# Two-layer transformer step on one core: modulation's end in item 22, items 29 to 31 reordered, attention transposed sooner, three context projections in the opening

## The reference

```python
# layer 0: 16 heads of 64
attn_in = _adaln(x, cond, ln1_w, ln1_b, g1_w, g1_b, b1_w, b1_b)
x = _attn(attn_in, attn_in, sa_wq, sa_wkv, sa_wo, sa_bo) + x     # with rope on q and k
cross_in = _adaln(x, cond, ln1_w, ln1_b, g1_w, g1_b, b1_w, b1_b)
ctx_n = _ln(context, ca_lnc_w, ca_lnc_b)
x = _attn(cross_in, ctx_n, ca_wq, ca_wkv, ca_wo, ca_bo) + x
ffn_in = _adaln(x, cond, ln2_w, ln2_b, g2_w, g2_b, b2_w, b2_b)
h = jax.nn.gelu(ffn_in @ ff_w1 + ff_b1, approximate=False)
x = h @ ff_w2 + ff_b2 + x
# layer 1: 16 heads of 8
mod = jax.nn.silu(c) @ W_ada + b_ada          # sh_msa, sc_msa, sh_x, sc_x, sh_mlp, sc_mlp
h1 = _modulate(_ln(x), sh_msa, sc_msa)
x = x + (attend(q, k, v of h1 @ W_qkv + b_qkv) @ W_proj + b_proj)
h2 = _modulate(_ln(x), sh_x, sc_x)
ctx = text_embed @ W_ctx + b_ctx
x = x + (attend(h2 @ W_q, ctx @ W_k, ctx @ W_v) @ W_out + b_out)
h3 = _modulate(_ln(x), sh_mlp, sc_mlp)
x = x + (gelu(h3 @ W_fc1 + b_fc1) @ W_fc2 + b_fc2)
```

## Time and profile before

| | us |
|---|---|
| median of three runs (393.54 to 394.5) | 393.87 |
| the profiled execution | 393.85 |
| its span in the profile | 392.1 |
| busy: TensorE | 375.7 (96%) |
| busy: VectorE | 305.3 (78%) |
| busy: ScalarE | 293.4 (75%) |
| busy: GpSimd | 177.5 (45%) |

### The profile page before, as it was taken

How to read it: one execution, slowest core, us unless ns; L and a number is a source line. 1 busy time by engine, 2 the same in 40 slices (tenths; PEclk the granted TensorE clock), 3 DMA queues, 4 the chain that set the end, 5 groups by cost and what they waited for, 6 DMA issues and landing times.

```text
span 392.1 us, 9870 instructions
## 1 busy us (share of the span) xinstructions
PE 375.7 (96%) x3591; PEld 287.5 (73%) x3591; DVE 305.3 (78%) x657; ACT 293.4 (75%) x1022; POOL 177.5 (45%) x156
## 2 busy tenths in 40 slices
PE   7999999999999999999999898999999999999997
PEld 3577777777877777777787577776768778788665
DVE  4779978979888888787898668674758888888751
ACT  2377878878878788777877585789679887987942
POOL 3165547557456665445575224342465650402120
PEclk9999999999999999999999899999999999999999
DMA  7153343223333333332122100000000000000001
GB/s 250 51 181 128 111 131 109 101 83 109 123 120 110 109 110 108 109 114 96 55 82 83 54 30 26 2 2 0 3 2 2 2 3 2 2 2 3 4 0 54
DMA packets 17424, 26.09 MB, mean 67 GB/s; under 512 B 3584, under 2 KB 6272, under 8 KB 17376
## 3 DMA queue, kind: packets, MB, share of 16 engines
q1 hardware_dynamic: 17088, 25.24, 19.0%
q10 hardware_dynamic: 288, 0.22, 0.3%
HBM read 8.67 MB, written 0.52 MB: 23 GB/s over the span
## 4 chain that ended last, share of the span: by engine, by line
PE 71%; DVE 15%; ACT 8%; issue 3%; POOL 2%; DMA 1%; DVEq 0%; POOLq 0%
PE bank L984 57%; PE bank L1065 7%; PE bank L1272 5%; ACT prob L437 3%; DVE nmax L847 2%; ACT raw L523 2%; DVE hT L668 1%; DVE nmax L719 1%; POOL xn L282 1%; DVE st L641 1%; DVE qk L751 1%; PE bank L1311 1%; PE bank L995 1%; DVE xn L656 1%; DVE x L636 1%
## 5 line engine op out<-in xcount | busy, mean ns | idle before, releaser
L301 POOL TENSOR_TENSOR swp<-swp,small 128x512 f32<-128x512 f32 x62 | 78.4, 1279 | 48.1 <-PE bank L984 28.3
L437 ACT ACTIVATE prob<-bank,nmax 128x128 f32<-128x128 f32 x256 | 91.5, 391 | 1.2 <-DVE nmax L719 1.2
L523 ACT ACTIVATE raw<-bank,nmax 128x128 f32<-128x128 f32 x256 | 72.7, 390 | 11.0 <-DVE nmax L847 10.9
L719 DVE TENSOR_REDUCE nmax<-bank 128x4 f32<-128x512 f32 x64 | 41.2, 685 | 29.7 <-PE bank L984 29.7
L437 ACT ACTIVATION_READ_ACCUMULATOR prob<-bank,nmax 128x1 f32 x256 | 59.2, 231 | 0.0
L334 POOL TENSOR_TENSOR prob<-prob,rz 128x512 f32<-128x512 f32 x29 | 30.2, 1041 | 55.1 <-DVE rz L724 55.1
L847 DVE TENSOR_REDUCE nmax<-bank 128x4 f32<-128x512 f32 x64 | 41.2, 684 | 15.4 <-PE bank L984 15.4
L984 PE MATMUL bank<-hT,wqkv 128*128 128x512 f32 x96 | 49.2, 596 | 0.5 <-DVE qk L751 0.5
L443 ACT ACTIVATE probT<-bank 128x512 f32<-128x512 f32 x32 | 19.1, 597 | 35.3 <-PE bank L1065 35.3
L751 DVE TENSOR_TENSOR qk<-bank,small 128x512 f32<-128x512 f32 x64 | 42.8, 670 | 0.9 <-ACT raw L428 0.6
L984 PEld LDWEIGHTS bank<-wqkv,oT 128*128 128x128 f32 x256 | 33.2, 192 | 14.0 <-issue 12.9
(11 more groups left out here) (114 smaller groups left out, 665.9 us busy)
## 6 DMA issues: line engine op xcount, KB each, us to landing
swp<-raw SPq DMA_DIRECT2D x124, 128.0 KB, 2.1
wqkv<-in_wqkv SPq DMA_DIRECT2D x16, 256.0 KB, 2.8
wff<-in_wff SPq DMA_DIRECT2D x4, 256.0 KB, 3.0
x<-in_x SPq DMA_DIRECT2D x2, 256.0 KB, 4.1
wmod<-in_wmod SPq DMA_DIRECT2D x1, 512.0 KB, 6.0
rows<-in_row SPq DMA_DIRECT2D x2, 192.0 KB, 2.4
ctx<-in_ctx SPq DMA_DIRECT2D x1, 384.0 KB, 3.1
ctxT<-in_ctxT SPq DMA_DIRECT2D x1, 384.0 KB, 3.4
```

The source lines that it names most:

```text
L301: nc.gpsimd.tensor_tensor(four(swp[:, m % 2, f, :]), four(swp[:, m % 2, f, :]), sin[f], ALU.mult).then_inc(rope_sin[f], 1)
L437: last = nc.scalar.activation(prob[:, hh, bcols(u)], S[hh][:, bcols(u)], ACT.Exp, bias=nmax[:, s % 2, hh, u:u + 1], accum_out=zsum[:, s % ...
L523: last = nc.scalar.activation(prob1[:, s % 2, hh, bcols(u)], score_bank(s, hh)[:, bcols(u)], ACT.Exp, bias=nmax[:, s % 2, hh, u:u + 1])
L719: nc.vector.tensor_reduce(nmax[:, s % 2, hh, :], four(S[hh][:, :]), AX.X, ALU.max, negate=True).then_inc(rowmax[hh], 1)
```

## The change

- **Modulation**: `modulation_end(1)` moves from item 28 to item 22, where VectorE calls it behind `rope_sum(23)`.
- **Context**: ctx1 of both halves and ck of half 0 are projected in the opening, where two idle matmuls stay of eight. ck of half 1, cv of half 0 and cv of half 1 take items 10, 18 and 26; items 9, 17 and 25 have none. ctxT and the two blocks of wsq that this needs are loaded behind the first half of x, as is now the first block of wmod.
- **Statistics**: of the four bn_stats in items 9, 17 and 25 two move to the next item, ahead of the aggregation.
- **Seam**: `prob_values(28)` and the transposition of item 29 now stand ahead of `down(0, 0, O)`; ScalarE copies item 28's result at the end of item 29; `down` waits for that copy, and the wait for the residual goes to `prob_values(29)`. `rope_sum(31)` moves from item 30 to the end of item 29, and VectorE's copy of transposed probabilities in item 30 between its two row maxima.
- **Attention**: `attention_T` stands ahead of the transpositions in items 11, 19 and 27, and ScalarE's copy of it ahead of the second head's exponentials.

The diff, cut to what is spoken of:

```diff
@@ -164,7 +164,7 @@
             sem(f"ld_{name}") for name in ("small", "tab", "rows", "ctx", "ctxT", "sq", "ff"))
-        ld_mod, ld_swap = pair("ld_mod"), sem("ld_swap")
+        ld_mod, ld_swap, ld_ctxw = pair("ld_mod"), sem("ld_swap"), sem("ld_ctxw")
         ld_wqkv = [sem(f"ld_wqkv{i}") for i in range(2 * RUN)]
@@ -194,10 +194,10 @@
                 ("q", 1), ("k", 1), ("cq", 0), ("cq", 1)]
-        PROJ_BANK = [O, O, O, O, O, O, X, Y, Y, W, S[1], S[1]]
+        PROJ_BANK = [O, W, O, O, O, O, X, Y, Y, W, S[1], S[1]]
         AT = {what: i for i, what in enumerate(PROJ)}
-        PROJ_SLOT = {9: 0, 10: 1, 17: 2, 18: 3, 25: 4, 26: 5}
+        PROJ_SLOT = {10: 3, 18: 4, 26: 5}
@@ -229,10 +229,8 @@
                     load(wqkv[:, s + 3, :], wqkv_in[:, s + 3, :], ld_wqkv[s + 3])
-                elif s == 5:
-                    load(ctxT[:, :, :], ctxT_in.rearrange("d (h t) -> d h t", h=2), ld_ctxT)
-                elif s <= 7:
-                    part = (slice(4 * P, len(SQ) * P), slice(0, 4 * P))[s - 6]
+                elif 5 <= s <= 7:
+                    part = (slice(6 * P, 8 * P), slice(0, 4 * P), slice(4 * P, 5 * P))[s - 5]
                     load(wsq[:, part], wsq_in[:, part], ld_sq)
@@ -243,6 +241,11 @@
             load_x(0)
+            load(wmod[:, 0:2 * P], wmod_in[:, 0:2 * P], ld_mod[0])
+            load(ctxT[:, :, :], ctxT_in.rearrange("d (h t) -> d h t", h=2), ld_ctxT)
+            for name in ("ctx", "ck"):
+                part = slice(SQ[name] * P, (SQ[name] + 1) * P)
+                load(wsq[:, part], wsq_in[:, part], ld_ctxw)
             load(wqkv[:, 0, :], wqkv_in[:, 0, :], ld_wqkv[0])
@@ -484,7 +487,7 @@
             def l0_slot(s):
-                if s >= 2:
+                if s >= 2 and s != 30:
                     evacuate_o(s - 2)
@@ -500,6 +503,8 @@
                     evacuate_v(s + 2)
+                if s == 29:
+                    evacuate_o(28)
                 if s == 28:
@@ -572,14 +577,13 @@
                     scale_shift(3, 1, Y)
+                if s % RUN == 3 and RUN < s:
+                    evacuate_attention(s // RUN - 1)
                 if s < ITEMS and s != 5:
...
             def background1(s):
-                for run in range(3):
-                    if s == RUN * run + 11:
-                        evacuate_attention(run)
                 if s == 3:
@@ -607,10 +611,12 @@
             load(small[:, 0:NFIRST], small_in[:, 0:NFIRST], ld_small)
-            load(wmod[:, 0:2 * P], wmod_in[:, 0:2 * P], ld_mod[0])
             act.wait_ge(ld_small, 16)
             nc.scalar.activation(silu[:, 0, :], condT, ACT.Exp, scale=-1.0).then_inc(exp_c, 1)
+            evacuate_proj("ctx1", 0)
+            evacuate_proj("ctx1", 1)
             scale_shift(0, 0, T[0])
+            evacuate_proj("ck", 0)
             evacuate_v(0)
@@ -636,8 +642,8 @@
-            def ln_stats(k, half):
-                for u in range(HALF):
+            def ln_stats(k, half, first=0, end=HALF):
+                for u in range(first, end):
                     last = nc.vector.bn_stats(st[:, half, u, :], x[:, HALF * half + u, :])
@@ -771,18 +777,22 @@
                 row_max(s, 0)
+                if s == 30:
+                    copy_T0(29)
                 row_max(s, 1)
...
                 middle0(s)
-                if s >= 1:
+                if s >= 1 and s != 30:
                     copy_T0(s - 1)
...
                 normalise(s)
-                if s < 31:
+                if s < 30:
                     rope_sum(s + 1)
+                if s == 22:
+                    modulation_end(1)
                 if s <= 28:
@@ -791,8 +801,10 @@
                 if s in (10, 18):
+                    ln_stats(1, s // RUN - 1, 2, HALF)
                     ln_aggregate(1, s // RUN - 1)
                 if s == 26:
+                    ln_stats(2, 0, 2, HALF)
                     ln_aggregate(2, 0)
@@ -801,7 +813,6 @@
                 if s == 28:
-                    modulation_end(1)
                     scale_shift_last(2, 0, O)
@@ -821,7 +832,7 @@
                     residual(run // 2, run % 2, W, wo_done, RUN * run + RUN)
-                    ln_stats(1 + run // 2, run % 2)
+                    ln_stats(1 + run // 2, run % 2, 0, 2)
                 if s in (10, 11, 18, 19):
@@ -832,6 +843,7 @@
                     ln_aggregate(3, 0)
+                    rope_sum(31)
                 if s == 30:
@@ -1082,7 +1094,7 @@
                     wait_hT(2, 0)
-                if s == 28:
+                if s == 29:
                     pe.wait_ge(x_sum[0], 3)
@@ -1116,8 +1128,10 @@
                 if i == 0:
-                    pe.wait_ge(ld_sq, 32)
+                    pe.wait_ge(ld_ctxw, 32)
                     pe.wait_ge(ld_ctxT, 16)
+                if i == 4:
+                    pe.wait_ge(ld_sq, 48)
                 if what in ("ck", "cv"):
@@ -1188,19 +1202,22 @@
                     fill(s + 2, 2)
-                if s == 29:
-                    background0(s)
                 if s == 31:
...
                     prob_values(s - 1)
+                if s == 29:
+                    prob_values(28)
                 transpose_probs(s, 0)
+                if s == 29:
+                    background0(s)
                 if s == 0:
                     pe.wait_ge(silu_done, 1)
+                    pe.wait_ge(proj_out, 3)
                     modulation(1, O)
-                if 1 <= s < 30:
+                if 1 <= s < 29:
                     prob_values(s - 1)
@@ -1215,7 +1232,7 @@
                 if s >= 2:
-                    pe.wait_ge(o_out, s - 1)
+                    pe.wait_ge(o_out, s if s == 29 else s - 1)
                 if s == 4:
@@ -1351,6 +1368,8 @@
                     project("cq", s // RUN - 1)
+                if s % RUN == 3 and RUN < s:
+                    attention_T(s // RUN - 1)
                 if 1 <= s <= ITEMS:
@@ -1366,8 +1385,6 @@
                         turn_back(2 * run + 1)
-                    if s == e + 11:
-                        attention_T(run)
                 if s == 1:
@@ -1426,8 +1443,11 @@
             modulation(0, Y)
-            keep_warm(8, X)
+            keep_warm(2, X)
+            project("ctx1", 0)
+            project("ctx1", 1)
             transpose_norm(0, 0, [T[0], T[1]])
+            project("ck", 0)
             pe.wait_ge(mod_read, 1)
```

## The result

The changed kernel takes 392.06 us (median of 11 runs, 391.11 to 393.91), the kernel before, beside it, 393.87 (11 runs, 393.54 to 395.94): a ratio of 0.9949, with an interval of 0.9929 to 0.9969. The forecast was 391.4, the range 389.0 to 393.3. The profiled executions have spans of 390.3 us after and 392.1 before, at mean granted clocks of 0.996 and 0.995, and each has one stretch of half clock of some 3.5 us, so they can be held against each other.

What follows compares the result with a forecast made beforehand. TensorE, with 71% of the chain that ends last, was taken as the bound. Terms of -2.6, +0.35, +1.35, -3.55, +0.1, +1.5, +1.3 and -0.9 sum to -2.45: from 393.85 to 391.4 us, range 389.0 to 393.3 (8 in 10).

Steps and rivals of the forecast that it cites:

- Bound: Whole kernel: TensorE carries 71% of the chain; edits count where they remove its matmuls or make or end its stops.
- Projections: Items 9, 17, 25: each loses a context projection of 0.86 us, nothing else being late there; -2.6 us in all.
- Opening: Before item 0: the projections taken in there delay the transpositions and ScalarE's hT; +0.35 us.
- rival of the late weights: Opening: context weights landing at 8.7, not 6.8, stop TensorE and halve the clock; 395.2 us, chance 0.06.
- Split statistics: Items 10, 18, 26: vare arrives 0.37 us later and waits for GpSimd's bias sum; 3 x 0.45 = +1.35 us.
- rival of the whole instruction: Items 10, 18, 26: VectorE and GpSimd exclude each other for whole instructions, so the product waits for pow; 392.3 us, chance 0.08.
- Modulation: Item 28: removing its last steps ends 1.78 us of TensorE's stop and 1.77 of half clock; -3.55 us.
- gives only its gap: Item 28: TensorE's stop shrinks but the clock still halves, so 1.77 us stay away; 393.2 us, chance 0.09.
- Seam: Items 29 to 31: later down and residual cost +1.5 us; half clock behind TensorE's 2.4 us stop costs +1.3.
- The clock holds in the seam: Items 29 to 31: TensorE's stop brings no half clock, so 1.3 us less, 390.1 us; chance 0.18.
- Attention: Layer 1, three runs of items: the earlier transposition brings VectorE's residual 0.3 us sooner each; -0.9 us.
- Item 22: The modulation's last steps cost VectorE 0.65 us there, mostly hidden by its wait for scores; +0.1 us.

Runs made afterwards that it cites:

- b: The changed kernel with the four bn_stats whole in items 9, 17 and 25, as before: 391.17 us, ratio 0.9933.
- c: The changed kernel with whole statistics and the order of items 29 to 31 as before: 388.82 us, ratio 0.9873.
- m: The changed kernel with items 29 to 31 ordered as before and GpSimd's bias sums moved from items 10, 18, 26 to 5, 20, 23: 390.43 us, ratio 0.9892.
- e: The changed kernel with GpSimd's bias sum put behind its pow in items 10, 18 and 26: 394.90 us, ratio 1.0022.
- h: The kernel before with only the three context projections moved to the opening: 393.43 us, ratio 0.9963.
- d: The kernel before with only the modulation's last steps moved from item 28 to item 22: 391.14 us, ratio 0.9941.
- k: The kernel before with eight idle matmuls in TensorE's stop in item 28 and nothing else: 393.23 us, ratio 0.9982.

## Why the prediction was right, and where it was off

The sign and the range held, and the forecast missed by 0.66 us. A part of this is luck. Two terms hung on a half clock that I took as certain: the gain of 1.77 behind item 28 and the loss of 1.3 in the seam. Each is there in a part of the executions only, and as their signs are opposite, the errors partly cancel. Without both terms the forecast would have been -1.98; the executions at full clock, 31 of before in the experiments' groups (median 393.12) and four of the changed kernel (391.61), lie 1.5 apart. Step by step:

- **Bound.** Right: what took matmuls off TensorE or changed one of its stops showed, and the copies that ScalarE lost in items 9, 17 and 25 did not.
- **Projections.** Right in size in items 9 and 25. Item 17 gave 0.69, since a late DMA of swp there pushed GpSimd's sine product against VectorE's product, which took 1.13 us and not 0.69. What failed is "nothing else is late there": in the kernels with whole statistics VectorE is the late one once TensorE is 0.86 sooner, and vare loses its lead in five of nine items.
- **Opening.** Right. One trace gives +0.45 at item 0; over the eleven kernels with the new opening the mean is 0.43, over the three with the old one 0.08, so 0.35. At item 9 this can't be told any more, for the first items differ by more than that between executions (last section). The rival of the late weights didn't happen: they landed at 6.84.
- **Split statistics.** The mechanism and nearly the size were right (0.55 an item, 0.45 forecast): in the changed kernel the split alone puts vare behind the bias sum's start, 0.52 us later where I had 0.37. But it isn't the only way there: the leaving projections do the same with whole statistics in about every second item, so the split isn't worth 0.45 when taken back, as b and c show. The rival of the whole instruction was wrong for the pow: the product begins 0.39 before its end and takes its usual 0.69 (91.10 to 91.79, the pow 90.47 to 91.49). It is right for the bias sum: vare (+0.02), the product in m (+0.54) and the rope sum in e (+1.08) all end after it, as if they had hardly run beside it. The Trainium skill (SBUF — State Buffer, Who interferes with whom) says whole instructions for both; the rows agree on the 128x512 bias sum and disagree on the 128x4 pow.
- **Modulation.** Right: 3.44 of 3.55, gap and clock, and "gives only its gap" was wrong for the profiled execution. But I took the slow clock as certain, for the trace showed one execution. It is 1.70 us in half of them. In medians the step is worth 2.5, not 3.5; that the profiled time (393.85) stood by chance on the median (393.87) hid it.
- **Seam.** Right: 1.76 for the queues where I had 1.5, 1.33 for the clock where I had 1.3, the stop 2.16 where I had 2.4. "The clock holds in the seam" is what some executions do, with a stop of the same 2.16; no run varied the stop's length.
- **Attention.** Mis-sized: project_attention starts 0.48 sooner behind its scores (1.10 us and not 1.58), and this comes through whole, as 0.50 at the next item's scores, with 0.1 given back two items later: 0.36 a run. I had let only the 0.30 before the residual count.
- **Item 22.** Nothing, where I had 0.1.

The 0.69 between -1.76 and -2.45 is made of 0.29 in the split statistics, 0.29 in the seam, 0.12 in the projections, 0.11 in item 28, 0.11 in items 12 and 13 and 0.04 in the opening, less 0.19 in layer 1 and 0.1 in item 22, with 0.02 of rounding.

## What to carry to other kernels

Where a step is taken off the engine that bounds an item, work out which engine is late next and what it now meets; here a gain of 0.86 brought VectorE's small instruction into GpSimd's way, and 0.5 was given back in five items of nine, with the statistics split in all. Price an edit of an order piece by piece: in the traces, half of the seam's reordering cost 3.7 us (1.3 of it by the clock), the other half gained 0.6, and only a kernel with one of them shows it. A number that hangs on the granted clock wants several executions, for one trace shows one side of a coin.

## What the runs showed of the hardware

- One and the same program runs in one execution with a stretch of half clock and in the next without (the kernel before: 34 of 65 with, 31 without). Stops of TensorE of the same length are followed by half clock in one trace and not in another: 1.92 us in before and 1.91 in h, 2.16 in the changed kernel and 2.16 in b. The stop of 0.98 us in the opening of before, and those of 0.71 and 0.91 in d's first items, left it at 1.00. The Trainium skill (TensorE: Matmul & The Clock Gate, Part 1: The HAM clock gate) calls the point at which the clock rises after a start run-variable, because the monitor isn't aligned with the kernel's start. The fall behind a stop varies likewise here; no run shows why.
- A 128x4 VectorE instruction of 0.17 us takes 0.98 to 1.28 when it arrives up to 0.32 us after a GpSimd sum of 128x512 has begun. Beside the same sum a rope sum of 1.21 takes 2.30 and a product of 0.69 takes 1.48. The pow of GpSimd is the one that gives way: 1.47 beside the end of the product and the rope sum in before, 2.03 beside the rope sum in the seam, and 1.02 in items 10, 18 and 26 of the changed kernel, where only a product begins near its end.
- The first items differ between executions of the same code: at item 9, with the kernel before as zero, d (the same code up to there) stood at +2.15 and k at +0.70. The waits are GpSimd's for the swapped halves (a stop of 1.79 us before item 2's sine product in d, 0.88 in before, both ended by the DMA of swp). That is as large as most parts of this change. Among the eleven kernels with the new opening, item 9 stands at +0.36 to +2.62.
